# Reordering the mean-square work in a state-space loop and the last row gathers of a decoder layer on one core

## What is computed

```
# 1. mixer: 32 heads of 64 channels, state size 128
proj = x @ Win.T                      # x_ssm, z, B, C, dt
xc, Bc, Cc = silu(causal_conv(...))   # 4 taps
h = exp(dt*A) * h + (dt*xc) outer Bc  # scan over 256 positions
y = einsum(h, Cc)
y = y * rsqrt(mean(y*y) + 1e-6) * silu(z)
x = layernorm(x + y @ Wout.T)
# 2. one of four experts, chosen by token id
x = layernorm(x + silu(x @ ctx[e].T) * (x @ ctx[e].T) @ ctx[e].T)
# 3. 16 experts, two per token by a router, and a shared one
out = sum_k w_k * swiglu(x, expert_k) + swiglu(x, shared)
x = layernorm(x + out)
```

## Time and profile before

| what | us |
|---|---|
| median of 3 runs | 667.09 |
| lowest and highest | 666.86, 670.83 |
| the profiled execution's own time | 666.86 |
| its span in the trace, first to last instruction | 665.1 |

### The profile page before, as it was taken

The page is one execution under the profiler, slowest core; times in us unless marked ns, Lnnn a source line. Parts: engine busy times, 40 slices in busy tenths (PEclk is TensorE's granted clock), DMA queues, the critical chain, the costliest instruction groups (busy, mean ns, idle before and its releaser), DMA issues.

```text
span 665.1 us, 12037 instructions
## 1 busy us (share of the span) xinstructions
PE 631.1 (95%) x3545; PEld 489.1 (74%) x3545; DVE 531.7 (80%) x851; ACT 453.6 (68%) x739; POOL 479.6 (72%) x458
## 2 busy tenths in 40 slices
PE   7989999999999999999999999999999999899961
PEld 6677888888878888788888887878888877444530
DVE  6999999999999999999999999948952658323253
ACT  3769788797887887978879788776423455333534
POOL 4396989879879898798887987596914647854463
PEclk9999999999999999999999999999999999999995
DMA  4261113112121131111211212042063493577443
GB/s 161 88 253 49 65 49 111 63 48 75 42 106 63 48 111 63 48 63 48 111 63 48 88 47 87 0 128 101 16 164 87 109 306 147 156 234 235 100 118 112
DMA packets 25994, 66.67 MB, mean 100 GB/s; under 512 B 4099, under 2 KB 16899, under 8 KB 23179
## 3 DMA queue, kind: packets, MB, share of 16 engines
q1 hardware_dynamic: 23131, 58.54, 26.2%
q0 software_dynamic: 2832, 7.75, 4.4%
HBM read 58.00 MB, written 9.85 MB: 102 GB/s over the span
## 4 chain that ended last, share of the span: by engine, by line
PE 81%; DVE 7%; issue 3%; ACT 3%; POOL 2%; another core or an unknown queue 1%; DMA 1%; POOLq 0%; ACTq 0%; DVEq 0%
PE ps L874 36%; PE ps L888 9%; PE ps L904 7%; PE ps L889 4%; PE ps L1168 4%; DVE conv L1723 4%; PE ps L806 3%; PE ps L824 3%; PE ps L1217 3%; PE ps L848 2%; PE ps L913 1%; PE ps L1142 1%; PE ps L914 1%; PE ps L1192 1%
## 5 line engine op out<-in xcount | busy, mean ns | idle before, releaser
L1723 DVE SCALAR_TENSOR_TENSOR conv<-ps,w_raw,conv 128x506 f32<-128x506 f32 (+3 forms) x352 | 320.5, 933 | 14.8 <-ACT conv L1368 8.4
L874 PE MATMUL ps<-x_hi,w_hi 128*128 128x512 f32 x384 | 158.0, 412 | 2.6 <-DVE x_lo L1644 1.5
L1368 ACT ACTIVATE conv<-ps,w_raw 128x512 f32<-128x512 f32 x160 | 108.4, 688 | 63.7 <-PE ps L874 63.1
L874 PE MATMUL ps<-x_hi,w_lo 128*128 128x512 f32 x384 | 151.3, 394 | 0.0
L874 PE MATMUL ps<-x_lo,w_hi 128*128 128x512 f32 x384 | 150.1, 391 | 0.0
L528 POOL TENSOR_TENSOR decay<-cum_b,cum_tok 128x512 f32<-128x512 f32 (+1 forms) x128 | 103.4, 829 | 9.1 <-DMA cum_b<-cum_scratch 9.1
L874 PEld LDWEIGHTS ps<-x_hi,w_hi 128*128 128x128 f32 x384 | 72.3, 188 | 20.6 <-issue 2.4
L534 POOL TENSOR_TENSOR decay<-decay,mask 128x512 f32<-128x512 f32 x64 | 82.7, 1292 | 5.0
L874 PEld LDWEIGHTS ps<-x_hi,w_lo 128*128 128x128 f32 x384 | 72.1, 188 | 16.8 <-DVE w_lo L1649 0.2
L874 PEld LDWEIGHTS ps<-x_lo,w_hi 128*128 128x128 f32 x384 | 72.4, 189 | 12.7
L1353 ACT ACTIVATE conv<-conv 128x1024 f32<-128x1024 f32 x80 | 79.3, 1059 | 1.5 <-DVE conv L1723 1.5
(11 more groups left out here) (286 smaller groups left out, 1107.7 us busy)
## 6 DMA issues: line engine op xcount, KB each, us to landing
cum_b<-cum_scratch SPq DMA_DIRECT2D x16, 1024.0 KB, 4.6
w_raw<-in_winT SPq DMA_DIRECT2D x15, 778.0 KB, 4.3
y_all<-in_wgu SPq DMA_DIRECT2D x4, 1408.0 KB, 12.8
late<-in_wdn SPq DMA_DIRECT2D x2, 1408.0 KB
x_scratch<-conv SPq DMA_DIRECT2D x19, 128.0 KB, 4.9
late<-in_woutT SPq DMA_DIRECT2D x1, 2048.0 KB, 8.4
ys_scratch<-y_blk SPq DMA_DIRECT2D x32, 64.0 KB
res_scratch<-conv SPq DMA_DIRECT2D x11, 130.0 KB
```

The source lines that it names most:

```text
L874: mm = pe.matmul(ps[:, tile_bank(n, tile) + hf, :], wp[:, par, w], xp[:, kk, t], start=(i == 0), stop=(i == 5))
L1368: act.activation(conv[:, par, tile, hf * 512:(hf + 1) * 512], ps[:, tile_bank(n, tile) + hf, :], ACT.Copy, scale=w_raw[:, par, tap:tap + 1 ...
L1723: dve.scalar_tensor_tensor(out=o[:, :, s:], in0=u[:, :, 0:T - s], scalar=w_raw[:, par, c:c + 1], in1=o[:, :, s:], op0=ALU.mult, op1=ALU.ad ...
```

## The change

Three things change in the loop, and three at the end.

- TensorE: `mix(r, 2)` and `mix(r, 3)` follow projection 1 instead of 3, `mean_square(r, 1)` follows projection 3 instead of 6.
- ScalarE: `square(r, 1)` goes with `work[1]`, ahead of the load of the activation table, and `rsqrt(r, 1)` with `work[6]`. POOL: `low_part(n - 2, 1)` comes ahead of `norm(n - 2, par, 0)`.
- VectorE: `gate(r, rp, 1)` and then `x_scaled(1)` come ahead of tap 0 of tile 1; `x_scaled(0)` waits for all mixes of the pair before.
- Gathers: the n-th waits for block 19 + n // 2 without the second bound. So gathers 8 and 9 wait for the projection of item 34, 10 and 11 for the `down` of item 33, and 12 to 15 for that of item 34.
- Both gathers of a block b >= 3 count on one semaphore, so `weigh_low(b)` waits for both.
- VectorE's last order: three `weigh_low` one item later, and then `weigh_high(b)` and `weigh_low(b + 3)` in turn. `LAST_ACT` is 3: ScalarE normalises three blocks, POOL three, VectorE two.

```diff
-LAST_ACT, LAST_POOL = 4, 6
+LAST_ACT, LAST_POOL = 3, 6
...
                 if tail:
+                    low_part(n - 2, 1)
                     norm(n - 2, par, 0)
-                    low_part(n - 2, 1)
...
-                j = BESIDE + min(n // 2, (n + 3) // 3)
+                j = BESIDE + n // 2
                 if j < NBLK:
                     pool.wait_ge(S["gu_done"], TBS + j + 1)
                 else:
-                    pool.wait_ge(S["dn_done"], ITEMS - 1)
+                    pool.wait_ge(S["dn_done"], min(TBS + j - 1, ITEMS))
...
-                sem = ld_y[b] if k == 1 else ld_row[NX + b] if b < HOISTED else ld_row[b]
+                sem = ld_row[NX + b] if k == 0 and b < HOISTED else ld_y[b]
...
-                    if tail and j == 3:
+                    if tail and j == 1:
                         mix(r, 2)
                         mix(r, 3)
+                    if tail and j == 3:
+                        mean_square(r, 1)
                     if mid:
                         for k in {4: (0, 1), 6: (2,), 7: (3, 4), 9: (5, 6)}.get(j, ()):
                             score(k)
-                    if tail and j == 6:
-                        mean_square(r, 1)
...
                 if tail:
-                    work[3] += [lambda: rsqrt(r, 0), lambda: square(r, 1)]
+                    work[1] += [lambda: square(r, 1)]
+                    work[3] += [lambda: rsqrt(r, 0)]
...
-                    work[7] += [lambda: rsqrt(r, 1)]
+                    work[6] += [lambda: rsqrt(r, 1)]
...
-                    ge(dve, S["y_done"], q * UNITS - (4 if c == 0 else 0))
+                    ge(dve, S["y_done"], q * UNITS)
...
+                if tail:
+                    between.setdefault((1, 0), []).append(lambda: gate(r, rp, 1))
                 if mid:
-                    between.setdefault((1, 1), []).append(lambda: x_scaled(1))
-                if tail:
-                    between.setdefault((1, 2), []).append(lambda: gate(r, rp, 1))
-                if mid:
+                    between.setdefault((1, 0), []).append(lambda: x_scaled(1))
...
-                    dve.wait_ge(ld_row[b], 16 + 16 * ((NBLK - 1 - b) // NX + 1) + 16)
+                    dve.wait_ge(ld_y[b], 32)
...
-                dve.wait_ge(ld_y[b], 16)
+                dve.wait_ge(ld_y[b], 16 if b < HOISTED else 32)
...
             for i in range(TBS, ITEMS):
-                if i == ITEMS - 2:
+                if i == ITEMS - 1:
                     for b in range(HOISTED):
                         weigh_low(b)
-                if i == ITEMS - 1:
-                    for b in range(LEADING):
-                        weigh_high(b)
                 gate_block(i)
...
-            for b in range(HOISTED, TB):
-                weigh_low(b)
-            for b in range(LEADING, TB):
+            for b in range(TB):
                 weigh_high(b)
-            for b in range(LAST_POOL, TB):
-                last_norm(b)
+                if b + HOISTED < TB:
+                    weigh_low(b + HOISTED)
+                if b == TB - 1:
+                    for c in range(LAST_POOL, TB):
+                        last_norm(c)
```

## The result

The changed kernel takes 675.94 us in the median of 8 executions (673.14 to 679.26), the kernel before beside it 668.3 us (666.85 to 676.89, 8 executions). The ratio is 1.0112, with a 95% interval of 1.0081 to 1.0143: slower, as forecast; the ratio itself is over 1%, though its interval begins at 0.8%. The profiled execution took 673.76 us; its span is 672.0 us, against 665.1.

What follows compares the result with a forecast made beforehand. TensorE bounds the loop; a chain of row gathers, weighing, norms and stores bounds the end. Profiled 666.86 + 4.4 (loop) + 2.9 (end) = 674.2, or 674.4 against the median; range 669.0 to 679.0, the forecast's own 672.3 to 676.5.

Steps and rivals of the forecast that it cites:

- The total: Whole kernel: 674.4 us against the median; slower 0.56, within 1% 0.41, faster 0.03.
- The loop: Projection loop: late transposes delay VectorE, so TensorE waits 0.31 us in each of 14 steps, 4.4 us in all.
- The cover of ScalarE's copy: Loop step: ScalarE's second copy, after projection 3, ends by 226.8, before the tap at 227.11; 0.3 us to spare.
- The end: After the last `down`: later gathers, then VectorE's lows, highs and norms, put the last store at about 663.7, +2.9 us.
- The landing of a gather: Kernel's end: a row gather lands 2.95 us after it starts, taken from the trace.
- Gather 12: Kernel's end: goes out at 651.1 and lands at 654.05, when `weigh_low(4)`, waiting for it, can start.
- (a): Rival, loop: slack hides VectorE's 0.64 us lateness and only the end counts; 670.0 us, chance 0.20.
- (b): Rival, end: VectorE's idle 2.34 us comes again on its path, before high 4; 676.7 us, chance 0.15.
- (c): Rival, loop: nothing absorbs the 0.64 us per step, needing a second chain from ScalarE to VectorE; 679.0 us, chance 0.07.
- (d): Rival, end: row gathers cause ScalarE's 3.34 us idle, and holding gathers 10 to 15 removes it; 666.7 us, chance 0.06.

Runs made afterwards that it cites:

- the shorter tap: The changed kernel with tap 1 of tile 1 over half its batches, leaving out half of that tap's sums; 668.92 us, step 27.00 us.
- the first group: Runs of kernels with the loop's edits alone, the end's edits alone, earlier second transposes, or a shortened tap, beside the kernel before at 668.78 us.
- the pacing alone: The kernel before with only the new waits of the gathers (10 and 11 behind the last but one `down`, 12 to 15 behind the last); 659.47 us against 659.18.
- the third group: Runs that include VectorE's last order alone, that order with norms shared 3, 2, 3, and the whole change again, beside the kernel before at 659.19 us.
- all gathers last: The kernel before with all 16 row gathers behind the last `down`, measured twice; 676.89 and 679.66 us against 659.2.
- the second group: Runs that include only the mix early, only the gathers' new waits, and only norms shared 3, 2, 3, beside the kernel before at 659.18 us.

## Why the prediction was right, step by step

**The total.** Forecast 674.4, measured 675.94, inside the range and slower, as the forecast was: +7.3 forecast, +7.6 by the medians. That it is so close is in part luck. In the profiled pair the loop's term is 0.6 us too small and the end's 2.4 too large (2.9 against 0.5), and 1.4 us come from elsewhere: 1.0 from a later first load that no edit touches and 0.4 between the loop and the first row gather, which was not looked into.

**The loop: mechanism right, term too small.** The forecast was 0.31 us per step and 4.4 in all; it is 0.355 and 5.0. The transposes were put at 226.50, which is 229.67 on the new scale, and they end at 229.66. VectorE then starts 0.15 us later; the prediction let it start at the very end of the transposes. That hand-over is the missing piece: most of it is still there at the third `weigh`, which was due at 234.50 + 3.17 = 237.67 and comes at 237.77. TensorE's stall falls on `score(4)` rather than on projection 8 behind it; the prediction named both places and worked out the second. That lateness of VectorE is what TensorE pays, and that it can be hidden if VectorE has 0.5 us less to do, is shown by the shorter tap.

**The cover of ScalarE's copy: a point that the sum didn't show.** The prediction called the second copy covered, "with 0.3 us to spare", and looked at it only after the wait for the transposes. ScalarE's timeline after:

```profile
227.49 1.28 ACT L1428 ACT_TABLE_LOAD   x1
228.78 1.27 ACT L1368 ACTIVATE conv<-ps,w_raw 128x512 f32<-128x512 f32 x2
```

The two copies end at 230.05, and the tap takes the result at 230.41: the margin of 0.36 us is real. But it exists only because VectorE is late already. With the transposes out of the way the same tap waited 1.00 us. The cause of the loop's loss is therefore the early mix, which delays two things at once, and not the place of the transposes alone. The prediction had both, but priced the copy only behind the wait for the transposes and never without it.

**The end: order right, size too large in the first group.** Forecast +2.9; in the profiled pair +0.5 net between first gather and end of span (6.4 to 6.9), and +0.8 [-1.5, +3.2] for the end's edits alone. From the last `take_y` on the working holds: it put 13.0 us from there to the last store (650.69 to 663.7), and the trace has 668.2 - 655.56 = 12.6, where before it was 10.15. The lows from row 4 and the highs were put at 8.3 us and took 667.06 - 658.86 = 8.2. What failed is the start of that sum: it kept the last `take_y` where it was, and by the first row gather that came 1.5 us sooner. Before, ScalarE sat 3.34 us, and TensorE sat for 3.70 us and then ran the last but one `down` at the half clock, in its timeline and in the table by stretch (columns as above):

```profile
645.56 0.68 PE L1217 MATMUL ps<-late,h_T 88*64 x1 [3.70 <-issue]
```

```profile
645.50:647.40 1.90, 1.84 (x8) 0.77 (x8) 0.60 (x2) 1.22 (x1) 0.95 (x1) 0.50 0.54 140
```

After, in ScalarE's and TensorE's timelines and in the table by stretch:

```profile
649.40 0.38 ACT L1557 ACTIVATE y_blk<-ps 128x256 f32<-128x256 f32 x1 [1.88 <-remote]
650.80 0.38 ACT L1540 ACTIVATE h_T<-ps 88x256 f32<-88x256 f32 x1 [1.02 <-remote]
```

```profile
651.32 0.42 PE L1217 MATMUL ps<-late,h_T 88*64 x1 [3.18 <-ACT h_T L1540]
```

```profile
651.30:652.30 1.00, 0.98 (x8) 0.50 (x8) 0.00 (x0) 1.00 (x1) 0.00 (x0) 0.99 0.36 124
653.50:655.30 1.80, 1.76 (x8) 0.79 (x8) 0.00 (x0) 0.00 (x0) 1.09 (x2) 0.50 0.48 150
```

The last two rows are eight matmuls each, the `down` of items 33 and 34: 1.0 us at 2.4 GHz and 1.8 at 1.2 GHz. Before, both ran at the lower level, 0.50 in the row above and again from 648.60 to 650.40. So of the 1.5 us TensorE's shorter pause gives 3.70 - 3.18 = 0.5 and the clock 0.9: the transposes behind the `down` of item 33 start at 652.33 instead of 647.47, which is 4.9 late, where that `down` itself was 5.8 late. The clock part is luck that no forecast could have, and it doesn't come with every execution of these edits. Four traces of the first group have the change's end: TensorE sat 3.18 and 3.33 us in two of them and then ran at full clock, 3.35 and 3.37 in the other two and then ran at half. Both traces with the old end have 3.70 us and the half clock. From the last `take_y` to the end of the span the four have 16.0 to 16.6 us, the two 14.4.

In the other two groups, where those stretches are missing, the end costs what was forecast, but not by the way that was forecast. From the first row gather to the end of the span it is 32.7 us with the whole change (630.9 to 663.6) and 29.7 with the old end, so 3.0 more, each from one trace. VectorE's order with the shared semaphore alone has 32.3, the pacing alone 29.8. The prediction did not split its 2.9; it began the sum with the later gathers and let the order follow. There the order costs by itself, with the gathers where they were; in the first group the parts weren't taken apart.

**The landing of a gather** was taken as 2.95 us. On the path that decides it is 3.41 (653.95 to 657.36), and 3.36 for the whole change in the third group; for the same gather, other traces with this order have 2.77 to 3.84 us to VectorE's start. An estimate by the formula of the Trainium skill (DMA: Bandwidth & Descriptors, section on the anatomy of one DMA) gives 2.3; the shortest landing of a row gather in the traces here is 2.7. Gather 12 was taken to be the one that VectorE waits for. It is gather 11, because row 3 shares a semaphore too. That the sum from the last `take_y` came out is again partly luck: gather 11 goes out 1.85 us ahead of gather 12 and lands 0.5 later than taken, and a low and a high (1.47 us) follow it before `weigh_low(4)` at 658.86. Gather 12 with the 2.95 us of the prediction would have given 655.80 + 2.95 = 658.75, nearly the same.

**The rivals.** (a) The loop absorbs it: refuted by the step of 27.32. (b) VectorE's idle 2.34 us comes again on its path: it did not; ahead of the last norms the longest wait between 657.39 and 667.06 us is 0.14 us. (c) Nothing absorbs the lateness: refuted, 0.355 and not 0.64 per step; the second chain that it needs exists, but its copy is ready 0.36 us before VectorE takes it. (d) The gathers cause ScalarE's idle stretch: it didn't shrink by the 2.9 us that this rival needs. Ahead of `take_y(32)` and the copy behind it ScalarE sat 3.34 us before and 1.88 + 1.02 = 2.9 after, and TensorE's pause is shorter by 0.3 to 0.5 us in all four traces with the change's end. So some part may belong to the edits. Whether gathers cause the stretch itself is open, since all gathers last was measured only where it is missing.

## What to carry to other kernels

When work is moved ahead of several things on the engine that sets the time, list everything behind it that another engine waits for, and price each as if the others were in time: two waits that are late for one reason hide each other, and taking one away shows nothing. A consumer that is released late and then has no gap passes on its lateness less the slack at the next place where the bounding engine needs it; a probe that shortens the consumer by half a microsecond tells this apart from a cost of the order itself. At the end of a kernel, idle time ahead of the last transfer is the place for all work that doesn't need it. An engine's fixed order together with a semaphore shared by an early and a late transfer took that work out of it here.

## What the runs showed of the hardware

The same kernel before took 668.78 us in one group of runs and 659.18 and 659.19 in two others, though the loop's step is 26.96 us in all three. Most of the difference falls into the last blocks: the first row gather starts at 628.69 in the trace of before and at 627.75 in that of the kernel with the new pacing in the second group, the last `take_y` at 650.69 and 643.00. Only the traces of the first group show ScalarE or VectorE idle for some 3 us with a releaser that the profile calls remote, as in this row of the kernel with the loop's edits alone, in the chain of waits, where VectorE is the one that sits:

```profile
639.91 3.21 another core or an unknown queue
```

What it waits for was not found. TensorE's granted clock after a pause went two ways: 3.18 and 3.33 us of idle time left it at 0.99 and 1.00, 3.35, 3.37 and twice 3.70 us before the same matmuls had left it at 0.50. SP issues the last stores in order, one every 0.4 to 0.5 us when they are due together: before, POOL's second norm ends at 659.96, its store goes at 659.98, and the last one, two stores on, at 660.84, though VectorE's norms were through at 659.4. After the change no store stands in front: VectorE's last norm ends at 668.15 and the last store goes at 668.18.
